# Cross attention: two PSUM banks for turned probabilities and two for value products, in place of three and one

## The chip, the cores and the metric

The kernel runs on one core of a Trainium2 chip. The metric is the time of one execution on the device, in microseconds (us), as a median of several runs. TensorE does the matrix products and the transposes, and writes only into PSUM, which has eight banks of 128 partitions x 512 f32 each. ScalarE (ACT in the rows) and VectorE (DVE) read those banks and write SBUF. GpSimd is POOL in the rows, and SyncE (SP) issues the DMAs.

## The reference, cut to what matters

The model is a stack of six layers on 16 batches of 64 tokens, 512 features wide. The change lies in the fourth, a cross attention without weights of its own: 16 heads of 32 features, the keys and the values are both the context itself (512 rows per batch).

```python
def _L1_xattn_ref(query, key, value):          # query: layer norm of x; key = value = ctx
    Q = query.reshape(B, Sq, H, D).transpose(0, 2, 1, 3)      # B 16, Sq 64, H 16, D 32
    K = key.reshape(B, Skv, H, D).transpose(0, 2, 1, 3)       # Skv 512
    V = value.reshape(B, Skv, H, D).transpose(0, 2, 1, 3)
    scores = jnp.einsum('bhqd,bhkd->bhqk', Q, K) / jnp.sqrt(jnp.asarray(D, Q.dtype))
    weights = jax.nn.softmax(scores, axis=-1)
    out = jnp.einsum('bhqk,bhkd->bhqd', weights, V)
    return out.transpose(0, 2, 1, 3).reshape(B, Sq, E)
...
x = x + _L1_xattn_ref(_layernorm(x, axis=-1), ctx_1024, ctx_1024)
```

## The kernel before

The program is written out by hand, a block for each layer, with a barrier of all engines between blocks. The function `cross_attention` is the block of the change. It works in 32 steps k, called quads below (the code counts them with `QUADS`); two quads make a batch b = k // 2. A quad has four tiles r = 0..3 of 128 rows (two heads x 64 tokens) by 512 keys. What happens to a quad:

- `scores(k)`, L1090, TensorE: 16 products into the four banks `score[0..3]` (banks 0 to 3), one bank for each tile r. It waits until the maxima of quad k-1 have read those banks.
- `scored_max(k)`, L1224, VectorE: four instructions, each copies a score bank to SBUF (`l1x_prob`) and takes the row's extreme.
- `exponential(k, r)`, L1175, ScalarE: the softmax's exponential, in SBUF.
- `turn_probabilities(k, r)`, L1105, TensorE: four 128x128 transposes of a tile into a `probt` bank. With n = 4k + r, before uses bank 4 + n % 3.
- `turned_copy(k, r)`: copies that bank to SBUF (`l1x_PT`). ScalarE (L1183) copies r = 0 and 2, and r = 1 of odd quads. VectorE (L1232) copies r = 3, and r = 1 of even quads.
- `half_product(k)`, L1125, TensorE: 64 small products with the values into columns 0 to 255 of the bank `pv` (bank 7 before). Two quads fill it.
- `heads_copy(b)` (L1188, ScalarE) copies these columns to SBUF, `turn_back(b)` (L1135, TensorE) transposes them into columns 256 to 511 of the same bank, and `finish_heads(b)` (L1247, VectorE) divides by the row sums, with a reciprocal (L1238) ahead of it.

Nothing is scheduled by a planner: each engine runs its own list in the written order and waits at semaphores. TensorE's order for quad k is: tiles 0 and 1 turned, in odd quads from 3 on `turn_back` of the batch before, scores of quad k+1, tiles 2 and 3 turned, product of quad k-1. VectorE's order for quad k is:

```python
if k > 0:
    turned_copy(k - 1, 3)
if k % 2 == 1 and k > 1:
    finish_heads(k // 2 - 1)
if not copied_by_scalar(k, 1):
    turned_copy(k, 1)
if k + 1 < QUADS:
    scored_max(k + 1)
if k % 4 == 3 and k > 4:
    moments(k // 4 - 1)
```

So the copy of tile 3 of a quad stands on VectorE behind the four maxima of the next quad and, in every fourth quad, behind `moments` (L1256) too, a statistic for the next layer norm.

Of the kernel before, what the change touches and what calls it, by code (L numbers as in the profile page):

```python
# [12 lines left out]
ACT = mybir.ActivationFunctionType  # L13
AX = mybir.AxisListType

P = 128
B, T, D = 16, 64, 512
KEYS = 512
TOK = B * T
# [1012 lines left out]
def cross_attention(nc, g, d, w, loads, zeros):  # L1032
# [8 lines left out]
    stats_done, aggr_done, var_eps, std_done, rstd_done = s_("stats"), s_("aggr"), s_("var_eps"), s_("std"), s_("rstd")  # L1041
    normed, rows_turned, rows_copied = s_("normed"), s_("rows_turned"), s_("rows_copied")

    score, probt, pv = g.bank[0:4], g.bank[4:7], g.bank[7]
    ctx_dram = context(d)
    final = TILES - 1
    last_summed, last_stats, last_aggr, last_eps, last_std, last_rstd, last_normed, last_turned, last_copied = (
# [4 lines left out]
    with nc.Block() as block:  # L1052
# [24 lines left out]
        @block.tensor  # L1077
        def _(pe):
            def scores(k):

                b, half = k // 2, k % 2
                if half == 0:
                    pe.wait_ge(keys_loaded[b % 3], 16 * (b // 3 + 1))
                if k > 0:
                    pe.wait_ge(scored, 4 * k)
                for e in range(2):
                    c = 2 * half + e
                    for r in range(4):
                        rows = slice(32 * r, 32 * r + 32)
                        last = nc.tensor.matmul(score[r][e * T:(e + 1) * T, :], w.QT[rows, c, b * T:(b + 1) * T],  # L1090
                                                w.KT[b % 3][rows, c, :], start=True, stop=True)
                last.then_inc(score_full, 1)

            def turn_probabilities(k, r):

                n = 4 * k + r
                if n == 2:
                    pe.wait_ge(last_summed, 1)
                pe.wait_ge(exp_done, n + 1)
                if n >= 3:  # L1100
                    pe.wait_ge(scalar_copied, SCALAR_COPIES[n - 3])
                    if VECTOR_COPIES[n - 3] > 0:
                        pe.wait_ge(vector_copied, VECTOR_COPIES[n - 3])
                for kc in range(KC):
                    last = nc.tensor.transpose(probt[n % 3][:, kc * P:(kc + 1) * P], prob(k, r)[:, kc * P:(kc + 1) * P],  # L1105
                                               g.ident[:, :])
                last.then_inc(probt_full, 1)

            def half_product(k):

                b, half = k // 2, k % 2
                pe.wait_ge(scalar_copied, SCALAR_COPIES[4 * k + 3])
                pe.wait_ge(vector_copied, VECTOR_COPIES[4 * k + 3])
                if k == 0:
                    pe.wait_ge(last_copied, 1)
                if half == 0:
                    pe.wait_ge(ctx_loaded[b % 4], 16 * (b // 4 + 1))
                    if b > 0:
                        pe.wait_ge(heads_done, b)
                for e in range(2):  # L1120
                    c = 2 * half + e
                    for kc in range(KC):
                        for r in range(4):
                            h = head_of(half, e, r)
                            last = nc.tensor.matmul(pv[32 * r:32 * r + 32, c * T:(c + 1) * T],  # L1125
                                                    w.ctx[b % 4][:, kc, h * HD:(h + 1) * HD],
                                                    turned(k, r)[:, kc * P + e * T:kc * P + (e + 1) * T],
                                                    start=kc == 0, stop=kc == KC - 1)
                last.then_inc(half_full, 1)

            def turn_back(b):

                pe.wait_ge(heads_out, b + 1)
                for half in range(2):
                    last = nc.tensor.transpose(pv[:, 256 + half * P:256 + (half + 1) * P],  # L1135
                                               w.headsT[b % 2][:, half * P:(half + 1) * P], g.ident[:, :])
                last.then_inc(heads_back, 1)

            def turn_last_rows():

                pe.wait_ge(last_normed, 1)
                for c in range(CH):
                    ins = nc.tensor.transpose(pv[:, c * P:(c + 1) * P], g.XN[:, final, c * P:(c + 1) * P], g.ident[:, :])
                ins.then_inc(last_turned, 1)

            scores(0)
            for k in range(QUADS):
                turn_probabilities(k, 0)
                turn_probabilities(k, 1)
                if k % 2 == 1 and k > 1:  # L1150
                    turn_back(k // 2 - 1)
                if k + 1 < QUADS:
                    scores(k + 1)
                turn_probabilities(k, 2)
                turn_probabilities(k, 3)
                if k > 0:
                    half_product(k - 1)
                else:
                    turn_last_rows()
            half_product(QUADS - 1)  # L1160
            turn_back(B - 1)
            pe.wait_ge(scored, 4 * QUADS)
            for t in range(EARLY_TILES):
                pe.wait_ge(normed, t + 1)
                for c in range(CH):
                    last = nc.tensor.transpose(score[t][:, c * P:(c + 1) * P], g.XN[:, t, c * P:(c + 1) * P], g.ident[:, :])
                last.then_inc(rows_turned, 1)

        @block.scalar
        def _(act):  # L1170
            def exponential(k, r):

                b, p = k // 2, 4 * (k % 2) + r
                act.wait_ge(scored, 4 * k + r + 1)
                nc.scalar.activation(prob(k, r)[:, :], prob(k, r)[:, :], ACT.Exp, scale=-1.0, bias=w.negmax[:, p:p + 1],  # L1175
                                     accum_out=w.rowsum[:, b % 4, p:p + 1]).then_inc(exp_done, 1)

            def turned_copy(k, r):

                act.wait_ge(probt_full, 4 * k + r + 1)  # L1180
                if r == 0 and k > 1:
                    act.wait_ge(half_full, k - 1)
                nc.scalar.activation(turned(k, r)[:, :], probt[(4 * k + r) % 3][:, :], ACT.Copy).then_inc(scalar_copied, 1)  # L1183

            def heads_copy(b):

                act.wait_ge(half_full, 2 * b + 2)
                nc.scalar.activation(w.headsT[b % 2][:, :], pv[:, 0:256], ACT.Copy).then_inc(heads_out, 1)  # L1188

            act.wait_ge(last_eps, 1)  # L1190
            nc.scalar.activation(g.rstd[:, 1, final:TILES], g.rstd[:, 0, final:TILES], ACT.Sqrt).then_inc(last_std, 1)
            for k in range(QUADS):
                exponential(k, 0)
                exponential(k, 1)
                if k % 2 == 1 and k > 1:
                    heads_copy(k // 2 - 1)
                turned_copy(k, 0)
                exponential(k, 2)
                if copied_by_scalar(k, 1):
                    turned_copy(k, 1)  # L1200
                exponential(k, 3)
                turned_copy(k, 2)
                if k == 0:
                    act.wait_ge(last_turned, 1)
                    nc.scalar.activation(w.QT[:, :, final * P:TOK], pv[:, :].rearrange("p (c n) -> p c n", c=CH),
                                         ACT.Copy, scale=-SCALE).then_inc(last_copied, 1)
            act.wait_ge(var_eps, 1)
            nc.scalar.activation(g.rstd[:, 1, 0:EARLY_TILES], g.rstd[:, 0, 0:EARLY_TILES], ACT.Sqrt).then_inc(std_done, 1)
            heads_copy(B - 1)
            for t in range(EARLY_TILES):  # L1210
                act.wait_ge(rows_turned, t + 1)
                nc.scalar.activation(g.XNT[:, :, t * P:(t + 1) * P], score[t][:, :].rearrange("p (c n) -> p c n", c=CH),
                                     ACT.Copy).then_inc(rows_copied, 1)

        @block.vector
        def _(dve):
# [10 lines left out]
            def turned_copy(k, r):  # L1227

                dve.wait_ge(probt_full, 4 * k + r + 1)
                if k > 1:  # L1230
                    dve.wait_ge(half_full, k - 1)
                nc.vector.tensor_copy(turned(k, r)[:, :], probt[(4 * k + r) % 3][:, :]).then_inc(vector_copied, 1)  # L1232

            def finish_heads(b):

# [9 lines left out]
                for e in range(2):  # L1245
                    rows = slice(e * T, (e + 1) * T)
                    last = nc.vector.tensor_tensor(  # L1247
                        w.heads[t % 2][tokens, :].rearrange("p (a e r n) -> p a e r n", a=2, e=2, r=4)[:, :, e, :, :],
                        pv[rows, 256:512].rearrange("p (a r n) -> p a r n", a=2, r=4),
                        w.rinv[b % 2][rows, :].rearrange("p (a r) -> p a r", a=2).unsqueeze(3).to_broadcast([T, 2, 4, HD]), ALU.mult)  # L1250
                last.then_inc(heads_done, 1)

# [2224 lines left out]
```

## Time and profile before

| | |
|---|---|
| median of 3 runs | 1443.33 us (1442.46 to 1444.77) |
| time of the profiled execution | 1442.41 us |
| its span in the profile | 1440.6 us |
| mean granted TensorE clock | 0.973 of 2.4 GHz |
| busy, share of the span | TensorE 92%, VectorE 73%, ScalarE 41%, GpSimd 11% |
| the block of the change | about 1048 to 1222 us of the span |

The span is measured in the profile from the first to the last instruction; the time on the device is 1.8 us longer in that execution. A busy share is a mean over six layers with different limits. For the change only the 174 us of its block count. There the rows of single instructions tell more than a share: an instruction's start, how long it ran, and in brackets how long its engine had been idle before it, and what ended that.

### The profile page before, as it was taken

The page shows a single profiled execution, that of the slowest core. Times are in us where ns is not written, and L with a number is a line of the kernel's source. Part 1 is how long each engine was busy: PE and PEld are TensorE (multiplying, and loading weights), DVE is VectorE, ACT ScalarE, POOL GpSimd, SP SyncE. Part 2 cuts the span into 40 slices and gives each one's busy share as a digit, 9 for nine tenths or more (in the row PEclk, how much of TensorE's full clock was granted, in tenths as well). Part 3 has the DMA queues.
Part 4 walks back from the last instruction along what each step waited for, and adds up shares of the span by engine and source line. Part 5 has one row for each costly group of instructions (what it writes and reads, how often), then busy time and mean ns, then how long its engine had stood idle before and what let it go on. Part 6 is the DMA issues. An engine that isn't in the chain of part 4 may idle for free. (4 is left out here: it accounts for less than half of the span.)

```text
span 1440.6 us, 31760 instructions
## 1 busy us (share of the span) xinstructions
PE 1331.5 (92%) x13487; PEld 934.8 (65%) x13498; DVE 1053.6 (73%) x2056; ACT 597.6 (41%) x1260; POOL 161.8 (11%) x109
## 2 busy tenths in 40 slices
PE   8999999999999999899989878999889898977898
PEld 5677777777777777334555667888756565465343
DVE  5477777778788778774577767867667787476787
ACT  2354444444444444121313442222278887143343
POOL 3200000000000000031000040000000000354630
PEclk9999999999999999799999998999989999999999
DMA  7243333433444423500004100000245563300000
GB/s 267 97 150 102 121 113 129 132 121 124 143 136 159 141 91 109 171 1 1 2 3 163 81 1 1 0 0 1 117 178 214 198 225 74 164 3 2 8 23 30
DMA packets 45960, 136.58 MB, mean 95 GB/s; under 512 B 10958, under 2 KB 11726, under 8 KB 39292
## 3 DMA queue, kind: packets, MB, share of 16 engines
q1 hardware_dynamic: 45820, 134.56, 26.9%
q8 instruction: 107, 1.75, 0.5%
q14 instruction: 33, 0.27, 0.1%
HBM read 117.47 MB, written 17.07 MB: 93 GB/s over the span
## 5 line engine op out<-in xcount | busy, mean ns | idle before, releaser
L777 ACT ACTIVATE l0x_prob<-l0x_prob,l0x_negmax 128x512 f32<-128x512 f32 x128 | 91.0, 712 | 173.9 <-DVE l0x_negmax L844 173.9
L635 PE MATMUL bank<-l0x_ctxT,l0x_upper_k 128*128 128x512 f32 x256 | 106.7, 417 | 1.3 <-PEq L311 1.3
L648 PE MATMUL bank<-l0x_upper_v,l0x_ctxT 128*128 128x512 f32 x256 | 104.7, 409 | 0.0
L650 PE MATMUL bank<-l0x_upper_v,l0x_ctxT_lower 128*128 128x512 f32 x256 | 100.9, 394 | 0.0
L637 PE MATMUL bank<-l0x_ctxT,l0x_lower_k 128*128 128x512 f32 x256 | 100.8, 394 | 0.0
L649 PE MATMUL bank<-l0x_lower_v,l0x_ctxT 128*128 128x512 f32 x256 | 100.6, 393 | 0.0
L636 PE MATMUL bank<-l0x_ctxT_lower,l0x_upper_k 128*128 128x512 f32 x256 | 100.4, 392 | 0.0
L1224 DVE CUSTOM_DVE_ANT_0 l1x_prob<-bank,l1x_zeros 128x512 f32<-128x512 f32 x128 | 80.8, 687 | 16.2 <-PE bank L1090 16.2
L1175 ACT ACTIVATE l1x_prob<-l1x_prob,l1x_negmax 128x512 f32<-128x512 f32 x128 | 91.0, 715 | 0.0
L1105 PE MATMUL bank<-ident,l1x_prob 128*128 128x128 f32 x512 | 79.6, 290 | 11.3 <-ACT l1x_prob L1175 9.6
L1105 PEld LDWEIGHTS bank<-ident,l1x_prob 128*128 128x128 f32 x512 | 56.4, 145 | 50.0 <-ACT l1x_prob L1175 42.3
L1448 POOL TENSOR_TENSOR tm_mixed<-tm_mixed,XNT 128x512 f32<-128x512 f32 x16 | 21.8, 1382 | 585.9 <-DVE tm_mixed L1495 585.9
L770 ACT ACTIVATE l0x_KT<-bank,columns 128x512 f32<-128x512 f32 x64 | 43.7, 683 | 100.1 <-PE bank L637 100.1
L844 DVE CUSTOM_DVE_ANT_0 l0x_prob<-bank,l0x_mask 128x512 f32<-128x512 f32 x128 | 80.7, 686 | 5.5 <-PE bank L663 5.5
L787 ACT ACTIVATE l0x_PT<-bank 128x512 f32<-128x512 f32 x128 | 65.6, 599 | 14.5 <-PE bank L672 14.5
L672 PE MATMUL bank<-ident,l0x_prob 128*128 128x128 f32 x512 | 63.1, 274 | 0.8 <-ACT l0x_prob L777 0.4
L635 PEld LDWEIGHTS bank<-l0x_ctxT,l0x_upper_k 128*128 128x128 f32 x256 | 48.1, 188 | 24.3 <-issue 14.2
L648 PEld LDWEIGHTS bank<-l0x_upper_v,l0x_ctxT 128*128 128x128 f32 x256 | 48.4, 189 | 22.6 <-issue 13.0
L672 PEld LDWEIGHTS bank<-ident,l0x_prob 128*128 128x128 f32 x512 | 57.5, 141 | 7.5 <-ACT l0x_prob L777 3.6
L835 DVE TENSOR_TENSOR l0x_ctxT_lower<-l0x_whole,l0x_ctxT 128x512 fp32r<-128x512 f32 x60 | 41.0, 684 | 20.6 <-ACT l0x_ctxT L762 20.4
L1183 ACT ACTIVATE l1x_PT<-bank 128x512 f32<-128x512 f32 x80 | 47.5, 594 | 19.4 <-PE bank L1105 18.3
L637 PEld LDWEIGHTS bank<-l0x_ctxT,l0x_lower_k 128*128 128x128 f32 x256 | 48.0, 187 | 11.3
(364 smaller groups left out, 3092.1 us busy)
## 6 DMA issues: line engine op xcount, KB each, us to landing
l0x_whole<-in_turned_context SPq DMA_DIRECT2D x16, 1024.0 KB, 5.4
l1x_KT<-in_turned_context SPq DMA_DIRECT2D x16, 1024.0 KB, 7.2
l1x_ctx<-in_ctx SPq DMA_DIRECT2D x16, 1024.0 KB, 4.8
fp_weight<-l0x_weight_piece SPq DMA_DIRECT2D x24, 352.0 KB, 4.5
f_raw<-fp_weight SPq DMA_DIRECT2D x3, 2816.0 KB, 18.6
l0x_abs_piece<-in_L_ffn_w_gate SPq DMA_DIRECT2D x16, 512.0 KB, 4.4
l0x_abs_piece<-in_L_ffn_w_up SPq DMA_DIRECT2D x16, 512.0 KB, 5.3
l0x_abs_piece<-in_L_ffn_w_down SPq DMA_DIRECT2D x16, 512.0 KB, 4.1
```

The source lines that it names most:

```text
L635: nc.tensor.matmul(bank[:, :], w.upper_k[:, kc, cols], c, start=kc == 0, stop=False)
L636: nc.tensor.matmul(bank[:, :], w.upper_k[:, kc, cols], c_lower, start=False, stop=False)
L637: last = nc.tensor.matmul(bank[:, :], w.lower_k[:, kc, cols], c, start=False, stop=kc == CH - 1)
L648: nc.tensor.matmul(bank[:, :], c, w.upper_v[:, kc, :], start=kc == 0, stop=False)
L649: nc.tensor.matmul(bank[:, :], c, w.lower_v[:, kc, :], start=False, stop=False)
L650: last = nc.tensor.matmul(bank[:, :], c_lower, w.upper_v[:, kc, :], start=False, stop=kc == CH - 1)
L672: last = nc.tensor.transpose(score[r][:, kc * P:(kc + 1) * P], w.prob[r][:, kc * P:(kc + 1) * P], g.ident[:, :])
L777: nc.scalar.activation(w.prob[r][:, :], w.prob[r][:, :], ACT.Exp, scale=-1.0, bias=w.negmax[:, p:p + 1], accum_out=w.rowsum[:, b % 2, p:p ...
L844: nc.vector.tensor_tensor_reduce(w.prob[r][:, :], score[r][:, :], w.mask[b % 2][:, :], 1.0, 3e38, ALU.add, ALU.min, w.negmax[:, p:p + 1]). ...
L1105: last = nc.tensor.transpose(probt[n % 3][:, kc * P:(kc + 1) * P], prob(k, r)[:, kc * P:(kc + 1) * P], g.ident[:, :])
L1175: nc.scalar.activation(prob(k, r)[:, :], prob(k, r)[:, :], ACT.Exp, scale=-1.0, bias=w.negmax[:, p:p + 1], accum_out=w.rowsum[:, b % 4, p: ...
L1224: nc.vector.tensor_tensor_reduce(prob(k, r)[:, :], score[r][:, :], w.zeros[:, :], 1.0, 3e38, ALU.add, ALU.min, w.negmax[:, p:p + 1]).then_ ...
```

## The change

Eight banks stay eight. The turned probabilities take banks 4 and 5 by turns (n % 2) in place of 4, 5 and 6. The value products and the turned-back heads take bank 6 for even batches and bank 7 for odd ones, in place of bank 7 for all. Two waits of TensorE change with that: tile n may be turned when tile n-2 has been copied out (before: n-3), and the first product of batch b may start when the heads of batch b-2 are finished (before: b-1). No instruction is added, removed or moved; each engine has the same list in the same order.

```diff
-    score, probt, pv = g.bank[0:4], g.bank[4:7], g.bank[7]
+    score, probt = g.bank[0:4], g.bank[4:6]
+    pv = lambda b: g.bank[6 + b % 2]
...
                 pe.wait_ge(exp_done, n + 1)
-                if n >= 3:
-                    pe.wait_ge(scalar_copied, SCALAR_COPIES[n - 3])
-                    if VECTOR_COPIES[n - 3] > 0:
-                        pe.wait_ge(vector_copied, VECTOR_COPIES[n - 3])
+                if n >= 2:
+                    pe.wait_ge(scalar_copied, SCALAR_COPIES[n - 2])
+                    if VECTOR_COPIES[n - 2] > 0:
+                        pe.wait_ge(vector_copied, VECTOR_COPIES[n - 2])
                 for kc in range(KC):
-                    last = nc.tensor.transpose(probt[n % 3][:, kc * P:(kc + 1) * P], prob(k, r)[:, kc * P:(kc + 1) * P],
+                    last = nc.tensor.transpose(probt[n % 2][:, kc * P:(kc + 1) * P], prob(k, r)[:, kc * P:(kc + 1) * P],
                                                g.ident[:, :])
...
                 if half == 0:
                     pe.wait_ge(ctx_loaded[b % 4], 16 * (b // 4 + 1))
-                    if b > 0:
-                        pe.wait_ge(heads_done, b)
+                    if b > 1:
+                        pe.wait_ge(heads_done, b - 1)
...
-                            last = nc.tensor.matmul(pv[32 * r:32 * r + 32, c * T:(c + 1) * T],
+                            last = nc.tensor.matmul(pv(b)[32 * r:32 * r + 32, c * T:(c + 1) * T],
...
-                    last = nc.tensor.transpose(pv[:, 256 + half * P:256 + (half + 1) * P],
+                    last = nc.tensor.transpose(pv(b)[:, 256 + half * P:256 + (half + 1) * P],
...
-                nc.scalar.activation(turned(k, r)[:, :], probt[(4 * k + r) % 3][:, :], ACT.Copy).then_inc(scalar_copied, 1)
+                nc.scalar.activation(turned(k, r)[:, :], probt[(4 * k + r) % 2][:, :], ACT.Copy).then_inc(scalar_copied, 1)
...
-                nc.scalar.activation(w.headsT[b % 2][:, :], pv[:, 0:256], ACT.Copy).then_inc(heads_out, 1)
+                nc.scalar.activation(w.headsT[b % 2][:, :], pv(b)[:, 0:256], ACT.Copy).then_inc(heads_out, 1)
...
-                nc.vector.tensor_copy(turned(k, r)[:, :], probt[(4 * k + r) % 3][:, :]).then_inc(vector_copied, 1)
+                nc.vector.tensor_copy(turned(k, r)[:, :], probt[(4 * k + r) % 2][:, :]).then_inc(vector_copied, 1)
...
-                        pv[rows, 256:512].rearrange("p (a r n) -> p a r n", a=2, r=4),
+                        pv(b)[rows, 256:512].rearrange("p (a r n) -> p a r n", a=2, r=4),
```

The last tile of rows that the block still has to turn for its queries (`turn_last_rows`, once, in quad 0) uses bank 6 in place of 7.

## Rows read from the trace of the kernel before

**Rows 1.** The page: span, and each engine's busy time, share and instructions.

```profile
span 1440.6 us, 31760 instructions
PE 1331.5 (92%) x13487; PEld 934.8 (65%) x13498; DVE 1053.6 (73%) x2056; ACT 597.6 (41%) x1260; POOL 161.8 (11%) x109
```

**Rows 2.** Stretches: length, busy us (instructions) by engine, PEclk granted, DMA share, GB/s.

```profile
1048.00:1222.00 174.00, 154.51 (x3124) 102.17 (x3124) 135.34 (x375) 144.99 (x361) 12.64 (x11) 0.96 0.50 181
...
1084.00:1088.00 4.00, 2.82 (x36) 1.27 (x24) 1.53 (x4) 2.31 (x7) 0.00 (x0) 1.00 0.47 188
1088.00:1092.00 4.00, 4.00 (x78) 3.28 (x77) 3.25 (x10) 2.39 (x6) 0.00 (x0) 0.68 0.01 4
```

**Rows 3.** Waits in 1048 to 1222: who, for whom, us in total, times, longest.

```profile
PEld bank L1105 <- ACT l1x_prob L1175: 42.3, 65, 4.0
ACT l1x_PT L1183 <- PE bank L1105: 18.3, 29, 2.4
DVE l1x_prob L1224 <- PE bank L1090: 16.2, 31, 3.2
```

**Rows 4.** TensorE in order of time, one batch: start, us, line, [idle before].

```profile
1066.33 1.11 PE L1090 MATMUL bank<-l1x_KT,XNT 32*64 32x512 f32 x16
...
1069.67 1.11 PE L1105 MATMUL bank<-ident,l1x_prob 128*128 128x128 f32 x8
1070.62 0.38 PE L1135 MATMUL bank<-ident,l1x_headsT 128*128 128x128 f32 x2
1070.93 1.11 PE L1090 MATMUL bank<-l1x_KT,XNT 32*64 32x512 f32 x16
...
1072.90 0.66 PE L1105 MATMUL bank<-ident,l1x_prob 128*128 128x128 f32 x4 [0.27 <-ACT l1x_prob L1175]
1073.48 1.10 PE L1125 MATMUL bank<-l1x_PT,l1x_ctx 128*32 128x64 f32 x64
1074.52 1.09 PE L1105 MATMUL bank<-ident,l1x_prob 128*128 128x128 f32 x8
1075.54 1.11 PE L1090 MATMUL bank<-l1x_KT,XNT 32*64 32x512 f32 x16
```

**Rows 5.** VectorE in the same batch.

```profile
1067.55 0.69 DVE L1224 CUSTOM_DVE_ANT_0 l1x_prob<-bank,l1x_zeros 128x512 f32<-128x512 f32 x1 [0.42 <-PE bank L1090]
...
1070.00 0.69 DVE L1232 COPY l1x_PT<-bank 128x512 f32<-128x512 f32 x1
...
1071.11 0.86 DVE L1247 TENSOR_TENSOR l1x_heads<-bank,l1x_rinv 64x256 f32<-64x256 f32 x2 [0.31 <-PE bank L1135]
...
1074.60 0.69 DVE L1232 COPY l1x_PT<-bank 128x512 f32<-128x512 f32 x1
```

**Rows 6.** ScalarE in the same batch, the copy of tile 2.

```profile
1072.74 0.60 ACT L1183 ACTIVATE l1x_PT<-bank 128x512 f32<-128x512 f32 x1
```

**Rows 7.** TensorE, the last scores of the block.

```profile
1208.21 1.11 PE L1090 MATMUL bank<-l1x_KT,XNT 32*64 32x512 f32 x16
```

**Rows 8.** VectorE in a quad with moments: the statistic, then two copies.

```profile
1096.95 0.69 DVE L1256 BATCH_NORM_STATS2 stats<-X 128x6 f32<-128x512 f32 x1
1097.56 1.27 DVE L1232 COPY l1x_PT<-bank 128x512 f32<-128x512 f32 x2
```

**Rows 9.** TensorE, interrupted or slow groups of the block.

```profile
1087.39 1.07 PE L1090 MATMUL bank<-l1x_KT,XNT 32*64 32x512 f32 x3 [1.18 <-issue]
...
1089.41 1.93 PE L1125 MATMUL bank<-l1x_PT,l1x_ctx 128*32 128x64 f32 x64
1091.28 1.85 PE L1105 MATMUL bank<-ident,l1x_prob 128*128 128x128 f32 x8
...
1127.94 0.38 PE L1125 MATMUL bank<-l1x_PT,l1x_ctx 128*32 128x64 f32 x10 [1.66 <-issue]
```

**Rows 10.** Another block: a VectorE result, and the TensorE group that waits for it.

```profile
1388.50 0.74 DVE L3154 SCALAR_TENSOR_TENSOR f_h<-bank,f_worth,f_silu 128x512 f32<-128x512 f32 x1
...
1389.29 0.55 PEld L3033 LDWEIGHTS bank<-f_gateT,f_x16T 128*128 128x128 bf16 x4
```

More of the change, by code:

```diff
@@ L1142, in turn_last_rows @@
                 for c in range(CH):
-                    ins = nc.tensor.transpose(pv[:, c * P:(c + 1) * P], g.XN[:, final, c * P:(c + 1) * P], g.ident[:, :])
+                    ins = nc.tensor.transpose(pv(0)[:, c * P:(c + 1) * P], g.XN[:, final, c * P:(c + 1) * P], g.ident[:, :])
                 ins.then_inc(last_turned, 1)
@@ L1204, in _ @@
                     act.wait_ge(last_turned, 1)
-                    nc.scalar.activation(w.QT[:, :, final * P:TOK], pv[:, :].rearrange("p (c n) -> p c n", c=CH),
+                    nc.scalar.activation(w.QT[:, :, final * P:TOK], pv(0)[:, :].rearrange("p (c n) -> p c n", c=CH),
                                          ACT.Copy, scale=-SCALE).then_inc(last_copied, 1)
```

## The prediction, made before the changed kernel ran

> **What bounds the kernel now.** The page first: TensorE is busy 92% of the 1440.6 us span [rows 1], but that is a mean over six layers, and the change touches one. So next the block alone: from 1048 to 1222 us TensorE is busy 154.5, VectorE 135.3 and ScalarE 145.0 of 174 us [rows 2]. Three engines near their limit and none at it: the block runs at the pace of a chain that goes from engine to engine. The waits say who waits for whom there: TensorE's weight loads for ScalarE's exponential, ScalarE's copies for the transposes, VectorE's maxima for the scores [rows 3]. None of them names the copies of turned tiles or the finished heads, the two things whose waits the change edits.
>
> Then one batch in order of time. Scores start at 1066.33, 1070.93 and 1075.54, so a quad takes 4.60 and 4.61 us and a batch 9.21 [rows 4]. From the scores at 1066.33 (of quad 3) to those at 1208.21 (of quad 31) lie 28 such intervals in 141.88 us [rows 4, 7]; at 4.61 they would take 129.1. The other 12.8 us are interruptions, like the 1.18 and 1.66 us that TensorE waited for "issue", its own instruction stream, and a short stretch at the lower clock [rows 9].
>
> **The changed waits, one by one.**
>
> *The products' bank.* The first product of a batch waited for the heads of the batch before. VectorE ends these at 1071.11 + 0.86 = 1071.97, the product starts at 1073.48 [rows 4, 5]. The wait was over 1.5 us early; moving it a batch back gives 0. Were the second bank worth something all the same, its outer bound is the whole idle time of TensorE ahead of tile 3 and of the product in that quad: from 1072.90 to 1073.48 it needs 0.42 for four loads (half of the 0.85 from tile 0 at 1069.67 less the start of the turning back), which leaves 0.16, and the 0.27 that the row puts down to the exponential: 0.43 x 15 batches = 6.5 us.
>
> *Tile 0* (waited for tile 1 of the quad before, now for tile 2). ScalarE copies that at 1072.74 + 0.60 = 1073.34; tile 0 starts at 1074.52 [rows 4, 6]. 1.2 us early, costs 0.
>
> *Tiles 2 and 3* (now for tiles 0 and 1 of their own quad). Where ScalarE copies them, the copy stands ahead of the exponential that the tile needs anyway. VectorE's copy of tile 1 comes ahead of its maxima, and TensorE turns tile 3 behind 1.1 us of scores and a tile. Costs 0.
>
> *Tile 1* (waited for ScalarE's copy of tile 2, now for VectorE's copy of tile 3 of the quad before). This is the term. Tiles 0 and 1 run as one group of eight from 1074.52 for 1.09 us, so tile 1 starts near 1074.95 [rows 4]. The copy it now needs starts at 1074.60 and ends at 1075.29 [rows 5]. It is late already in the old timetable, and it is late because it stands behind the four maxima of the next quad. That closes a ring through two engines: scores, four maxima, copy of tile 3, tile 1, the next scores. Its length:
> - scores start to first maximum: 1067.55 - 1066.33 = 1.22 [rows 4, 5];
> - first maximum to the copy: 1070.00 - 1067.55 = 2.45 [rows 5];
> - the copy itself 0.69 [rows 5];
> - VectorE's end to TensorE's start: in another block the result ends at 1389.24 and the load starts at 1389.29, 0.05 [rows 10]. Bounds: 0, and the 0.16 above;
> - tile 1 to the next start behind it: as from tile 3 at 1072.90 to the product at 1073.48, 0.58 [rows 4].
>
> Sum 4.99 us for a quad without turning back, against 4.61. With turning back, tile 1's loads take 0.42 and the turning back 0.31 of TensorE by its start and the scores' (1070.62, 1070.93), in the weight loads 0.42; I take 0.84 in place of 0.58: 5.25 against 4.60. A batch becomes 10.24, by 1.03 longer. The interval repeats 14 times each: 14 x 1.03 = +14.4 us. One more quad of the first kind lies ahead of 1066.33: +0.4.
>
> *Moments.* In every fourth quad VectorE runs the statistic between the maxima and the copy: 1097.56 - 1096.95 = 0.61 [rows 8]. Before nobody waited for what it pushed back; in the ring it counts in full. It is there seven times, the last after the last scores: 6 x 0.61 = +3.7 us.
>
> *What the ring hides.* Before, an interruption of TensorE anywhere lengthened the quad. Now TensorE waits ahead of tile 1: it would be there at 1069.67 + 0.42 = 1070.09, and is let go at 1070.69 + 0.05 [rows 4, 5], 0.65 us later. An interruption in tiles 2, 3, 0 or a product is hidden up to 0.65. Of the 28 intervals nine are 4.9 us or longer, seven with the extra in such a place (as the 1.66 in a product); two have it in the scores (1.18) or tile 1 [rows 9]. 7 x 0.65 = -4.6 us; bounds 0 and -12.8.
>
> *Ends.* The last quad has no scores behind its tile 1, and its tiles 2 and 3 wait for exponentials; ScalarE's list from the last scores on is as before: 0. The barrier behind the block passes the difference on in full, and nothing later depends on these banks.
>
> Sum: 14.4 + 0.4 + 3.7 - 4.6 = +13.9 us. The profiled execution took 1442.4 and becomes 1456.3; the median of the runs is 0.9 above it, so I forecast **1457.2 us** as the median, 1.0% slower. The 0.16 in place of 0.05 for the hand-over would add 29 x 0.11 = 3.2.
>
> The Trainium skill (Perfetto Trace Analysis, Matmuls) wants independent groups of products to rotate through different banks, so that emptying one overlaps the next. By that the products' second bank should gain; the rows above give it at most 6.5 us and most likely 0, and the same rule says what the transposes lose.
>
> **Rivals.**
>
> *More time at the lower clock.* TensorE now idles in each quad. What speaks for it: after the stretch 1084 to 1088, in which TensorE was busy 2.82 of 4 us, the next one shows a granted clock of 0.68 [rows 2], part of it at 1.2 GHz, and there the products took 1.93 in place of 1.10 and the eight transposes 1.85 in place of 1.09 [rows 4, 9]. Against: the ring leaves TensorE some 4.3 of 5 us busy. A visit costs 0.83 + 0.76 less the 0.65 of slack, near 1 us, and more where it meets the scores; six visits with scores slow too (some 1 us more) give +12: 1469. The Trainium skill (TensorE: Matmul & The Clock Gate, A second HAM failure mode) has this case: a kernel cycling PSUM banks that idles TensorE in small pieces swings between the two clocks. That the trace shows only one swing in the block speaks against it here.
>
> *The ring hides nearly all interruptions.* If what fills TensorE's instruction stream goes on while it waits, the 12.8 us vanish rather than 4.6: 1457.2 - 8.2 = 1449. For it: they do not depend on the data. Against: two lie where nothing hides them.
>
> *No change.* Tile 1's wait is met in time after all, as VectorE falls into another rhythm: 1443. It would need maxima 0.35 us earlier, while they start right behind the scores.
>
> *Faster.* The products' bank was what held TensorE ahead of tile 3 and the product, and tile 1's wait costs nothing: -6.5, 1436.8. It decides only if more than 2.9 us of the 6.5 come back and the ring costs under that. The rows name the exponential for the idle time, not the heads.
>
> **How the numbers follow.** The forecast 0.76, the clock 0.10, the hidden interruptions 0.08, no change 0.04, faster 0.02. The forecast's own range is 1452 to 1462 (hand-over +3.2, interruptions -4 to +4.6). For 8 in 10 I take in part of the neighbours: 1451 to 1465. A measurement of this kernel tells 0.2%, 2.9 us, from no change. Slower by more than that: 0.76 + 0.10 + 0.08 = 0.94; within it 0.04; faster 0.02.
>
> **What the profile after would show.** Tile 1 as a group of its own (x4, where eight ran together), idle ahead of it some 0.5 us, put down to VectorE's copy L1232 (its line there may be one lower), some 29 times; score starts 5.0 and 5.25 us apart, and 5.6 in the six quads behind moments; ScalarE's waits longer; products and heads as before. Wrong it would be if scores still come every 4.6 us, if the idle time stands ahead of tile 0 or of a product, or if the granted clock of the block falls well under 0.96.

## The result, and the profile after

The changed kernel takes 1448.61 us (median of 8 runs, 1444.96 to 1451.83) against 1443.67 us (8 runs, 1438.71 to 1447.87): ratio 1.0037, interval 1.0023 to 1.0052. It is slower, by 5 us where 14 were forecast, and under the range of 1451 to 1465 us.

The page after, beside [rows 1]:

```profile
span 1449.9 us, 31759 instructions
...
PE 1327.4 (92%) x13487; PEld 934.3 (64%) x13498; DVE 1052.9 (73%) x2056; ACT 597.7 (41%) x1260; POOL 161.5 (11%) x109
```

The busy times are the same; the difference is idle time. In this execution the span grew by 9.3 us, 6.75 of them between the scores of quad 3 and those of quad 31, 0.5 ahead of these in the block (the interval from quad 2 to quad 3, 5.06 in place of 4.59), 1.6 ahead of the block and 0.5 behind it. The parts outside of the block differ between executions: in the 14 profiles of this case its first scores start between 1047.4 and 1050.5 us.

TensorE after, by start, for the batch of [rows 4] (lines behind the edited ones are one higher, L1091 are the scores, L1106 the turned tiles):

```profile
1068.42 1.11 PE L1091 MATMUL bank<-l1x_KT,XNT 32*64 32x512 f32 x16
...
1072.93 0.63 PE L1106 MATMUL bank<-ident,l1x_prob 128*128 128x128 f32 x4 [0.75 <-ACT l1x_PT L1184]
1073.39 0.38 PE L1136 MATMUL bank<-ident,l1x_headsT 128*128 128x128 f32 x2
1073.70 1.11 PE L1091 MATMUL bank<-l1x_KT,XNT 32*64 32x512 f32 x16
...
1078.20 0.63 PE L1106 MATMUL bank<-ident,l1x_prob 128*128 128x128 f32 x4 [0.75 <-ACT l1x_PT L1184]
1078.76 1.11 PE L1091 MATMUL bank<-l1x_KT,XNT 32*64 32x512 f32 x16
```

Tiles 0 and 1, one group of eight before, are two groups of four, with 0.75 us of idle time ahead of tile 1. Scores start 5.28 and 5.06 us apart, where they were 4.60 and 4.61. What let tile 1 go is seen with VectorE's and TensorE's weight-load rows and ScalarE's copy of tile 0 beside them:

```profile
1072.09 0.69 DVE L1233 COPY l1x_PT<-bank 128x512 f32<-128x512 f32 x1
1072.33 0.59 ACT L1184 ACTIVATE l1x_PT<-bank 128x512 f32<-128x512 f32 x1
...
1072.89 0.42 PEld L1106 LDWEIGHTS bank<-ident,l1x_prob 128*128 128x128 f32 x4 [0.96 <-ACT l1x_prob L1176]
...
1077.37 0.69 DVE L1233 COPY l1x_PT<-bank 128x512 f32<-128x512 f32 x1
```

VectorE's copy ends at 1072.09 + 0.69 = 1072.78, and the weights of tile 1 are loaded from 1072.89, 0.11 later. The bracket of the product names ScalarE's copy, which ends at 1072.92, after the load began: with several semaphores to wait for, the name in the bracket is only the one that came last by the profile, and here it is the wrong one. The waits of the block (1048 to 1230 us), beside [rows 3], show the same in sum:

```profile
PEld bank L1106 <- ACT l1x_prob L1176: 38.5, 40, 4.0
ACT l1x_PT L1184 <- PE bank L1106: 28.7, 33, 1.8
PEld bank L1106 <- issue: 25.5, 26, 1.6
PE bank L1106 <- ACT l1x_PT L1184: 15.7, 21, 0.8
...
PE bank L1106 <- DVE l1x_PT L1233: 1.8, 3, 0.8
```

A quad with the statistic (L1257) is longer still: 1100.29 - 1094.64 = 5.65.

```profile
1094.64 1.11 PE L1091 MATMUL bank<-l1x_KT,XNT 32*64 32x512 f32 x16
...
1098.31 0.69 DVE L1257 BATCH_NORM_STATS2 stats<-X 128x6 f32<-128x512 f32 x1
1098.92 0.67 DVE L1233 COPY l1x_PT<-bank 128x512 f32<-128x512 f32 x1
1099.74 0.63 PE L1106 MATMUL bank<-ident,l1x_prob 128*128 128x128 f32 x4 [1.34 <-ACT l1x_prob L1176]
1100.29 1.11 PE L1091 MATMUL bank<-l1x_KT,XNT 32*64 32x512 f32 x16
```

So the ring is there, as long as forecast. What is not there is the interruptions. The 28 intervals sum to 148.63 us; 14 x (5.28 + 5.06) + 6 x 0.59 = 148.3 is the ring alone. Of the 12.8 us of interruptions of before 0.3 are left, where 8.2 had been expected to stay.

### The profile page after: what moved, and what is told of

Same layout as the page of the kernel before. It is cut to its first block and busy times, and to the rows that moved or that the text cites. A ratio compares the mean times of both kernels' runs of the same rounds, so it can differ in the third digit from the quotient of the medians.

```text
span 1449.9 us, 31759 instructions
## 1 busy us (share of the span) xinstructions
PE 1327.4 (92%) x13487; PEld 934.3 (64%) x13498; DVE 1052.9 (73%) x2056; ACT 597.7 (41%) x1260; POOL 161.5 (11%) x109
## 5 line engine op out<-in xcount | busy, mean ns | idle before, releaser
L1106 PE MATMUL bank<-ident,l1x_prob 128*128 128x128 f32 x512 | 78.1, 286 | 29.2 <-ACT l1x_PT L1184 15.7
L1106 PEld LDWEIGHTS bank<-ident,l1x_prob 128*128 128x128 f32 x512 | 55.6, 143 | 66.9 <-ACT l1x_prob L1176 38.5
L787 ACT ACTIVATE l0x_PT<-bank 128x512 f32<-128x512 f32 x128 | 65.6, 599 | 12.9 <-PE bank L672 12.9
```

The lines of the kernel that those rows point to most:

```text
L1106: last = nc.tensor.transpose(probt[n % 2][:, kc * P:(kc + 1) * P], prob(k, r)[:, kc * P:(kc + 1) * P], g.ident[:, :])
```

## The experiments

Three questions: is the ring the whole of the loss, and the second products' bank worth nothing; what were the interruptions; and why did they go. Each ratio is against runs of the kernel before on the same chip. "Block" is the time from the scores of quad 3 to those of quad 31: 141.88 us before, 148.63 after.

### Which of the two edits

**One wait alone** (wait_alone), in the kernel before (3 + 1 banks).

```diff
-                if n >= 3:
-                    pe.wait_ge(scalar_copied, SCALAR_COPIES[n - 3])
+                back = 2 if n % 4 == 1 else 3
+                if n >= back:
+                    pe.wait_ge(scalar_copied, SCALAR_COPIES[n - back])
...
```

> The kernel before with its three banks for turned probabilities and its one for products; only tile 1 of each quad waits for the copy of tile n-2 in place of n-3. The ring theory (scores, four maxima, copy of tile 3, tile 1; its slack hides TensorE's interruptions) expects the same timetable as in the changed kernel: scores 5.28 and 5.06 us apart by turns, 5.65 behind moments, 148.6 us from the scores at the start of the third interval to the last (141.9 before), no interruption on TensorE, +0.4% (+5 us). The rival, that the second products' bank takes part (a gain that paid for some of the ring), expects more than +0.6%, 10 us or above.

Measured: ratio 1.0052 (1.0036 to 1.0068), block 149.38 us, intervals of 5.06, 5.28 and 5.65 as in the changed kernel but for two (5.72 and 5.88), and no idle time ahead of a product that the rows call "issue". The wait of tile 1 alone makes the whole timetable; the other edited waits add nothing to it.

**One bank for products** (one_product_bank), in the changed kernel.

```diff
-    pv = lambda b: g.bank[6 + b % 2]
+    pv = lambda b: g.bank[7]
...
-                    if b > 1:
-                        pe.wait_ge(heads_done, b - 1)
+                    if b > 0:
+                        pe.wait_ge(heads_done, b)
```

> The changed kernel with one bank for products and heads again, and their old wait; two banks for turned probabilities stay, and a bank is left idle. Ring theory: products were never held by the heads, so the profile is that of the changed kernel, +0.4% (+5 us). If the second products' bank gives something back: slower than the changed kernel by up to 6.5 us, +0.8%.

Measured: 1.0053 (1.0036 to 1.0070), block 149.33. The interval overlaps that of the changed kernel, and all other quads are the same. The one that differs, 6.27, lies between the scores of quads 7 and 8, where the changed kernel has a longer one too (5.54 in place of 5.28) and the kernel before its longest, 8.17. The second products' bank shows no worth here.

**The statistic behind the copy** (moments_behind), in the changed kernel.

```diff
                 if k > 0:
                     turned_copy(k - 1, 3)
+                if k % 4 == 0 and k > 4:
+                    moments(k // 4 - 2)
...
-                if k % 4 == 3 and k > 4:
-                    moments(k // 4 - 1)
+            moments(QUADS // 4 - 2)
             early_variances()
```

> The changed kernel with the statistic of each fourth quad issued behind the copy of tile 3 in place of ahead of it. Ring theory: the six quads of 5.65 us become 5.06, block shorter by 3.5 us, so +0.1% against the kernel before in place of +0.4%. If the hidden interruptions come back with less slack, part of the 3.5 us is lost again. If the ring does not set the pace there, no difference to the changed kernel.

Measured: 1.0014 (0.9998 to 1.0029), block 145.30, all quads 5.06 or 5.28 but one (5.81). 3.3 us of the block go, as six times 0.59 say.

**The copy of tile 3 behind three maxima, or two** (copy_behind_3_after, copy_behind_2_after, copy_behind_3_before). Inside the loop over r of `scored_max`, behind the maximum r = 2 (r = 1 for two maxima); the copy at the head of the next quad goes.

```diff
                                                    ALU.add, ALU.min, w.negmax[:, p:p + 1]).then_inc(scored, 1)
+                    if k > 0 and r == 2:
+                        turned_copy(k - 1, 3)
...
-                if k > 0:
-                    turned_copy(k - 1, 3)
```

> The changed kernel (2 + 2 banks) with the copy of tile 3 behind three maxima in place of four, and so ahead of the statistic too. Ring theory: the ring shrinks by 0.61 to 4.4 and 4.65 us, a mean of 4.53, under the 4.61 of the old timetable; the old chain through ScalarE's exponentials binds again or both do. Clean quads take 4.6 to 4.75 us. The slack that hid the interruptions goes with it: if they come back in full (12 us), the time is that of the kernel before (within 0.2%); if they stay away, 28 x 0.45 = 12 us less, -0.8%.

> The changed kernel with the copy of tile 3 behind two maxima. The ring theory says it is not the bound here (3.8 to 4.0 us), so clean quads as before or as with three maxima, 4.6; the third and fourth maxima come 0.61 later and may hold ScalarE. Interruptions in full: within 0.3% of the kernel before. If quads are longer than 4.7 the maxima's delay is what counts.

> The kernel before (3 + 1 banks) with the copy of tile 3 behind three maxima. There the copy was not waited for at once, so the ring theory expects no gain and at most 0.05 us a quad from the fourth maximum coming later: within 0.2% of the kernel before. It also gives what the two splits of the banks are worth with the ring out of the way, beside copy_behind_3_after: equal, if the second products' bank is worth nothing.

Measured: in the changed kernel 1.0021 (1.0003 to 1.0039) behind three and 1.0002 (0.9983 to 1.0022) behind two; in the kernel before, behind three, 1.0006 (0.9992 to 1.0019). Undisturbed quads take 4.66 and 4.55, then 4.60 and 4.60: the ring is broken, the 4.61 of before are back. And the interruptions are back, mostly in the quads where they were before. The idle time called "issue" ahead of TensorE's products from 1068 to 1208 us (who, for whom, us in total, times, longest), first with the changed banks and the copy behind three maxima, then in the kernel before:

```profile
PE bank L1126 <- issue: 4.1, 5, 1.9
...
PE bank L1106 <- issue: 3.5, 2, 2.5
...
PE bank L1091 <- issue: 1.7, 2, 1.3
```

```profile
PE bank L1125 <- issue: 3.9, 4, 1.7
...
PE bank L1090 <- issue: 1.5, 2, 1.2
...
PE bank L1105 <- issue: 1.1, 1, 1.1
```

In the changed kernel the whole block has 0.7 us of it, at one place. The blocks are 145.0, 142.1 and 142.5 us. Against the changed kernel's 148.6 that is 4 and 7 us less, where the shorter ring alone would have given 20: 28 undisturbed intervals take 128.9 us, and the interruptions add 16 and 13. Against the kernel before nothing is gained.

### What the interruptions are

**Small loads** (small_loads_before, small_loads_after). The loads of keys and values inside the block bring 256 bytes in place of 1 MB, so these kernels leave out most of their input and compute with old contexts.

```diff
-                    sp.dma_start(w.KT[b % 3][:, :, :], d.ctxT[b + 3]).then_inc(keys_loaded[b % 3], 16)
+                    sp.dma_start(w.KT[b % 3][0:1, 0, 0:64], d.ctxT[b + 3][0:1, 0, 0:64]).then_inc(keys_loaded[b % 3], 16)
...
```

> The kernel before, but each load of keys and values inside the block (13 and 12 of 1 MB) brings 256 bytes only, at the same place and behind the same wait; so batches compute with old contexts. It asks what interrupts TensorE (the rows say only issue). If its instruction stream comes late because it shares the DMA engines with the 1 MB loads: the 12.8 us of interruptions go, all quads take 4.6, and the time falls by 10 to 13 us, -0.8%. If they have another cause (the stream is too slow for 200 small instructions in a quad whatever the loads do): they stay in the same quads, no change.

> The same small loads in the changed kernel. Ring theory: nothing to hide any more, but the ring is unchanged: quads of 5.06, 5.28 and 5.65 as in the changed kernel, 148.6 us less at most 0.5, +0.4% against the kernel before with its full loads. Beside small_loads_before it gives the ring's price without interruptions: 28 quads, near 18.5 us.

Measured: 0.9890 (0.9868 to 0.9912) in the kernel before, 1.0034 (1.0019 to 1.0050) in the changed one. The blocks are 128.99 and 148.36 us. The time of the kernel before fell by 15.5 us (1443.93 to 1428.47), and every one of its 28 quads now takes 4.59 to 4.62; 12.9 us went, all that had been called interruptions. So the 1 MB loads make them, and the ring's bare price is 148.36 - 128.99 = 19.4 us in the block.

TensorE's instructions are themselves loaded by DMA. From 1048 to 1222 us of the kernel before the queues carried:

```profile
q1 hardware_dynamic: 10336, 31.10, 49.2%
q8 instruction: 25, 0.41, 0.9%
```

That is 25 blocks of 16 KB. The single records of that queue in the trace have a block that ends 1.22 to 1.43 us before TensorE goes on from each of the seven interruptions of 0.35 us and more that the rows name "issue" (they sum to 6.5 us; the rest of the 12.9 is not named so). SyncE issues the 2 MB of a batch within 0.4 us, at one place in TensorE's program. Four of the 25 instruction blocks start within 0.1 us of the end of the last packet of such a pair of loads, as if they had stood behind it, and with the small loads no interruption is left. The Trainium skill (Runtime: NRT & Kernel Launch, Instruction fetch mechanics) gives the same 16 KB a block, and has the cost of crossing from one to the next mostly hidden. Here it was not: 12.9 us in 142.

### Why the ring hid them

**TensorE busy in place of waiting** (filled_before). The kernel before, with a product whose result is overwritten ahead of tile 1. The trace has it as two products of 128x512 and two weight loads.

```diff
+                if r == 1 and k > 0:
+                    nc.tensor.matmul(probt[n % 3][:, :], g.ident[:, :], g.rows[:, 0, :], start=True, stop=True)
                 for kc in range(KC):
                     last = nc.tensor.transpose(probt[n % 3][:, kc * P:(kc + 1) * P], prob(k, r)[:, kc * P:(kc + 1) * P],
```

> The kernel before (3 + 1 banks, 1 MB loads) with one more product of 128x512 ahead of tile 1 of each quad but the first, whose result is overwritten: TensorE is about 0.45 us longer in a quad, without waiting. It asks why the ring hid even interruptions far over its 0.65 us of waiting. If lateness is counted from the loads, so that a TensorE which gets to the place later finds its block there: quads of 5.1 to 5.2 without waiting, and most of the 12.8 us of interruptions gone. If the waiting at tile 1 is what hides them: quads of 5.1 plus the 10 to 12 us of interruptions again, about 13 us more in all than the kernel before.

Measured: 1.0047 (1.0033 to 1.0060), block 151.07; the quads of the block take 5.28 to 5.29 and 5.50 to 5.51 without exception, and nothing interrupts TensorE. The product cost more than I took, 0.79 us a quad ((151.07 - 128.99) / 28). From 1068 to 1208 us this kernel, and under it the changed one:

```profile
1068.00:1208.00 140.00, 138.97 (x2582) 87.17 (x2574) 106.45 (x292) 113.90 (x286) 7.70 (x6) 1.00 0.52 191
```

```profile
1068.00:1208.00 140.00, 117.31 (x2544) 78.40 (x2544) 107.22 (x294) 115.09 (x291) 7.70 (x6) 1.00 0.53 192
```

TensorE is busy 138.97 of 140 us in the one and 117.31 in the other. There is no waiting in the first that could hide anything, and the interruptions are gone all the same, at the same 191 GB/s. So the slack at tile 1 is not needed. There too four instruction blocks start within 0.1 us of the end of a pair of loads. What fits both kernels is that the loads set when a block comes, and that a TensorE which takes 5.1 us and more for a quad needs it later. It is no fixed time: in the kernel before the seven interruptions end 6.3 to 9.8 us after the first load of the pair nearest ahead was issued. One thing stays open. The added product also makes TensorE's list longer, so in filled_before the blocks begin at other instructions. That alone does not explain it, since the changed kernel keeps the old list and lost the interruptions too, but no run holds the two apart.

### The loads in pieces

In pieces_before, pieces_after and pieces_copy_behind_3: the same bytes, but one piece of 256 KB per turned tile, keys and values by turns, each piece behind the old wait too. The 25 loads become 100 pieces, 75 more DMAs and not the 96 of the expectation below.

```diff
-                    sp.dma_start(w.KT[b % 3][:, :, :], d.ctxT[b + 3]).then_inc(keys_loaded[b % 3], 16)
...
+                for step in range(8):
+                    kb, kc = (b - 1, 3) if step == 0 else (b, (step - 2) // 2)
+                    cb, cc = (b - 2, 3) if step == 1 else (b - 1, (step - 3) // 2)
+                    if step % 2 == 0 and 0 <= kb and kb + 3 < B:
+                        sp.wait_ge(score_full, 2 * (kb + 1))
+                        sp.wait_ge(probt_full, 8 * b + 1 + step)
+                        sp.dma_start(w.KT[kb % 3][:, kc, :], d.ctxT[kb + 3][:, kc, :]).then_inc(keys_loaded[kb % 3], 16)
...
-                    pe.wait_ge(keys_loaded[b % 3], 16 * (b // 3 + 1))
+                    pe.wait_ge(keys_loaded[b % 3], 16 + 64 * (b // 3))
```

> The kernel before with every load of the block whole in bytes, but cut in four pieces of 256 KB, one piece issued for each turned tile, in place of 2 MB issued within 0.4 us once in a batch. If TensorE's instruction blocks come late because they queue behind those 2 MB: most of the 12.8 us go, quads of 4.6, -0.6 to -0.8%, faster than both kernels. If what counts is the number of bytes in the block and not the burst: interruptions stay, no change. If the pieces' 96 more DMAs cost something themselves (late loads): quads longer than 4.6 with waits for the keys.

> The changed kernel with its loads in the same pieces. The ring sets the pace and the interruptions were hidden already: as the changed kernel, +0.3 to +0.5% against the kernel before. Beside pieces_before it gives the price of the split of the banks where nothing pays for it: 18 us, 1.3%.

> The changed banks (2 + 2), the copy of tile 3 behind three maxima, loads in pieces. The ring is out of the way and the interruptions too: as pieces_before, -0.6 to -0.8%. If the second products' bank were worth something, this would be the faster of the two.

Measured:

| kernel | median us | ratio (interval) | block us |
|---|---|---|---|
| before, pieces | 1429.87 | 0.9903 (0.9886 to 0.9920) | 130.53 |
| changed, pieces | 1448.71 | 1.0035 (1.0014 to 1.0056) | 148.37 |
| changed, copy behind three maxima, pieces | 1429.06 | 0.9895 (0.9878 to 0.9911) | 129.43 |

From 1068 to 1208 us of the first of them:

```profile
1068.00:1208.00 140.00, 132.95 (x2944) 89.96 (x2932) 121.52 (x339) 129.00 (x326) 9.23 (x8) 1.00 0.66 195
```

195 GB/s as before (192 in the changed kernel), spread evenly, and TensorE gets through 2944 products and transposes where the changed kernel reaches 2544. The number of bytes was not the matter, the burst was. The first and the third are faster than both kernels of this case, by 1.0% against the one before, and their intervals overlap. So do those of the two banks' splits with the copy behind three maxima and whole loads (1.0006 and 1.0021). With the copy early enough the runs do not tell 3 + 1 from 2 + 2 banks. Where nothing pays for the ring, the change costs 148.37 - 130.53 = 17.8 us in the block, and 1448.71 - 1429.87 = 18.8 us, 1.3%, in the time.

## Why the prediction was wrong

- **Tile 1's wait and the ring**: right, in mechanism and place. 4.99 and 5.25 were forecast, 5.06 and 5.28 measured. VectorE's end to TensorE's load is 0.11 us, not 0.05, and within its bounds; from that load to the scores it takes 0.81 with the turning back, not 0.84, and 0.59 without, not 0.58. Over the 28 intervals that is +15.7 us in place of +14.4, and for the one ahead of them +0.5 in place of +0.4.
- **Moments**: 0.59 x 6 = 3.5 us, forecast 3.7; shown by moving them, which took 3.3 us off the block.
- **The products' bank, tiles 0, 2 and 3**: nothing, as forecast; shown for the bank by one_product_bank, and for all of them together by wait_alone. The outer bound for the bank rests on a slip: from tile 0 to the turning back the rows have 1070.62 - 1069.67 = 0.95 us, not 0.85. The term was 0 either way.
- **What the ring hides**: this is the step that failed. I bounded what one interruption could lose by the 0.65 us for which TensorE would wait ahead of tile 1, and counted seven of nine: -4.6. Measured -12.5. The bound took an interruption for a fixed piece of work on TensorE. The runs show a block of instructions whose arrival the loads set: without the bursts the interruptions are gone or nearly so (small_loads_before, pieces_before), and a TensorE that is slower for another reason has none either, even in the scores and in tile 1, which I had excepted (filled_before). That all might vanish stood among the rivals with 0.08 and 1449 us, by an instruction stream that fills up while TensorE waits. The number came out, the reason only in half: in filled_before TensorE did not wait and the interruptions were gone as well. The count was off by one besides. Three of the nine lay in the excepted places, since the 6.01 us interval had its own in the scores, which by my rule would have given 6 x 0.65 = 3.9:

```profile
1179.59 1.10 PE L1090 MATMUL bank<-l1x_KT,XNT 32*64 32x512 f32 x11 [0.35 <-issue]
```

- **The sum**: 15.7 + 3.5 - 12.5 = +6.7 in the block, as the profile has it; with the 0.5 ahead of them +7.2. The medians of the runs say +4.9 us, and the two profiled executions +9.3. What makes up the difference outside of the block is open, so that the median falls within half a microsecond of the rival's 1449 is in part luck.
- **The lower clock**: no visit in these intervals. The granted clock from 1068 to 1208 us is 1.00 in the changed kernel. The one of before, at 1088, came behind the interruption of 1.18 us, and small_loads_before, which has no interruption, has 1.00 there too. It was not the only one of the block, as the prediction has it: in both kernels the granted clock is 0.50 (1.2 GHz) from 1052 to 1056 us, in the block's first quads, ahead of the intervals counted here. By the Trainium skill (TensorE: Matmul & The Clock Gate, A second HAM failure mode) it might have swung more often with an idle piece in each quad; the trace does not show it, with 117.31 us busy of 140.
- **The profile's marks**: eight as four and four, 5.06, 5.28 and 5.65 came as forecast. That the idle time would be put down to VectorE's copy did not: the rows name ScalarE or "issue" for most of it.

## What to carry to other kernels

When a bank is taken from a rotation, ask which instruction must now be done one step earlier, and what stands ahead of it on its engine's list; a copy behind another stage's work ties two engines into a ring. Idle time of TensorE that the profile calls "issue" in the midst of a group can be its own instructions coming late behind large loads: look at what the DMA queues carry just before, and issue the loads evenly before tuning anything else there. Such a loss is no constant: any change that makes the engine slower may seem to pay for itself by it, and any that makes it faster may seem to gain nothing.

## What the runs showed of the hardware that was not expected

- Loads of 1 MB for keys and values, two within 0.4 us, cost 12.9 us in 142 by holding up TensorE's instruction stream; the same bytes in 256 KB pieces cost 1.5 (130.53 against 128.99 us).
- The same loads do less to a slower TensorE: quads of 4.6 us were hit in nine of 28 cases, quads of 5.1 to 5.7 us in two at most, and in none where TensorE worked through (filled_before).
- A hand-over from VectorE's copy to TensorE's weight load took 0.11 us in this block; the 0.05 of another block was half of it.
